# First attention of a two-layer decoder: weight folds and weight splits put first, latent matmuls in two halves, half of the key spreads by vector copies, last chunk projected tile by tile

## The reference, cut to what matters

```
xn = layernorm(x)
q  = (xn @ Wq_d + bq_d) @ W_qk + b_qk        # 12 latents -> 32 heads x 4
kv = xn @ Wkv_d + bkv_d                      # 4 latents, the same for all heads
p  = softmax(q . kv / sqrt(4))               # per sequence: 64 x 64, 32 heads
v  = kv @ Wv_u + bv_u                        # 4 -> 32 x 16
x  = x + (p v) @ Wo + bo
```

## Time and profile before

| | us |
|---|---|
| median of 3 runs (1344.39 to 1349.4) | 1345.4 |
| the profiled execution | 1349.59 |
| its span | 1347.8 |
| stage A in it (to VectorE's last instruction) | 206.7 |

### The profile page before, as it was taken

One profiled execution on the slowest core, in us unless ns is written; L12 is line 12 of the kernel. 1 busy time (PEld: TensorE's weight loads), 2 busy tenths in 40 slices (PEclk: granted clock), 3 DMA queues, 4 the chain that ended last, 5 costly groups with the idle time before them and its releaser, 6 DMA issues. The chain is left out here.

```text
span 1347.8 us, 24381 instructions
## 1 busy us (share of the span) xinstructions
PE 1148.2 (85%) x9342; PEld 606.5 (45%) x9342; DVE 759.5 (56%) x1316; ACT 416.6 (31%) x654; POOL 393.5 (29%) x318
## 2 busy tenths in 40 slices
PE   4798873988896979998999999999488769999993
PEld 2455441666663434443444444444354334444441
DVE  6756652688876876437514313512499822646466
ACT  4556741555541113411111211211233212222230
POOL 3334535888840000049200000000122200225052
PEclk8888855799998998998999999999699979999997
DMA  5000001111101004322000000000000000000000
GB/s 193 4 3 4 21 2 31 42 40 41 42 5 39 0 11 123 111 72 88 0 0 1 0 0 0 1 0 0 13 10 10 3 24 1 9 23 23 8 32 32
DMA packets 30634, 35.82 MB, mean 27 GB/s; under 512 B 7194, under 2 KB 21811, under 8 KB 30548
## 3 DMA queue, kind: packets, MB, share of 16 engines
q1 hardware_dynamic: 29810, 34.56, 8.2%
q10 hardware_dynamic: 738, 0.05, 0.0%
HBM read 30.10 MB, written 4.19 MB: 25 GB/s over the span
## 5 line engine op out<-in xcount | busy, mean ns | idle before, releaser
L1641 DVE TENSOR_TENSOR d_h_low<-d_hf,d_h_high 128x512 f16<-128x512 f32 (+1 forms) x40 | 32.6, 816 | 205.9 <-ACT d_h_high L1698 205.9
L109 PE MATMUL d_p_up<-d_xt_high,wd_hi 128*128 128x512 f16 (+1 forms) x352 | 134.1, 381 | 2.9 <-PE d_p_y L111 1.5
L110 PE MATMUL d_p_up<-d_xt_low,wd_hi 128*128 128x512 f16 (+1 forms) x352 | 133.9, 380 | 0.0
L111 PE MATMUL d_p_up<-d_xt_high,wd_lo 128*128 128x512 f16 (+1 forms) x352 | 133.9, 380 | 0.0
L109 PE MATMUL d_p_y<-wd_hi,d_h_high 128*128 128x512 f16 (+1 forms) x272 | 104.7, 385 | 3.1 <-DVE d_h_low L1641 3.1
L110 PE MATMUL d_p_y<-wd_lo,d_h_high 128*128 128x512 f16 (+1 forms) x272 | 104.8, 385 | 0.0
L111 PE MATMUL d_p_y<-wd_hi,d_h_low 128*128 128x512 f16 (+1 forms) x272 | 104.6, 385 | 0.0
L404 POOL TENSOR_TENSOR a_pt_low<-a_ex,a_pt_high 128x1024 f16<-128x1024 f32 x32 | 68.1, 2128 | 99.0 <-ACT a_pt_high L786 99.0
L151 ACT ACTIVATE d_sg<-d_p_up 128x512 f32<-128x512 f32 (+1 forms) x40 | 23.7, 593 | 211.8 <-PE d_p_up L111 211.8
L1837 POOL MEMSET e_wskip<- 128x128 f32 x1 | 0.2, 205 | 300.1 <-POOLq L1567 300.1
L2172 DVE TENSOR_TENSOR f_h_low<-f_sq,f_h_high 128x512 f16<-128x512 f32 x32 | 27.4, 857 | 71.0 <-ACT f_h_high L2244 71.0
(11 more groups left out here) (304 smaller groups left out, 2978.6 us busy)
## 6 DMA issues: line engine op xcount, KB each, us to landing
wd_raw<-in_w_d SPq DMA_DIRECT2D x16, 616.0 KB, 3.7
wd_raw<-in_w_f SPq DMA_DIRECT2D x8, 578.0 KB, 3.7
X<-in_x SPq DMA_DIRECT2D x4, 1024.0 KB, 9.4
b_kt<-in_ctx_t SPq DMA_DIRECT2D x128, 32.0 KB
out_x<-wd_raw SPq DMA_DIRECT2D x16, 256.0 KB, 2.0
b_cd<-in_ctx SPq DMA_DIRECT2D x32, 64.0 KB, 2.3
a_bd<-a_keys SPq DMA_DIRECT2D x72, 4.0 KB
wd_raw<-in_w_c SPq DMA_DIRECT2D x4, 274.0 KB, 5.1
```

The lines of the kernel that those rows point to most:

```text
L109: nc.tensor.matmul(ps, st[0], mv[0], start=start, stop=False)
L110: nc.tensor.matmul(ps, st[0], mv[1], start=False, stop=False)
L111: return nc.tensor.matmul(ps, st[1], mv[0], start=False, stop=stop)
L1641: nc.vector.tensor_tensor(hid[1][0:n, d % NH, :], value, hid[0][0:n, d % NH, :], ALU.subtract).then_inc(h_ready, 1)
```

## The change

- **Loads.** The sync queue now fetches x chunk 0, `Wo`, `bo`, x chunk 1, all of `w_c` in one transfer (its buffer holds all four pieces), x chunks 2 and 3. `Wv_u` and `bv_u` go first on ScalarE's queue.
- **Folds.** They are written into `p_st` (free until the first scores_t), in pieces between the first chunk's T, L, V and Q; the splits stand among the first query splits on VectorE.
- **Fillers.** `keep_warm(k)` issues k f16 matmuls of 512 columns into unused partitions of `p_m`: 14 at the very start, then `light(c, j)` of them before turn_top in units with little chunk work: 4, 2, 2, 2, 2 in units 2 to 6, 4 in each of units 10, 18, 23, 24, 25, 26 and 31 (54 in all).
- **Latents.** The four matmuls of L (chunks 1 to 3) are two in the unit's place and two after the following turn_top.
- **Key spreads.** Of 8 heads, 4 are written by VectorE (two copies after the peak of units j = 3 and 4, 12 in all) and 4 by 12 transfers for each chunk.
- **Weights of stage C** are split before the unit loop: ScalarE's four passes before its copy of L, VectorE's four after the first two norms of chunk 1.
- **Last chunk.** Z and O of chunk 3 become `Y` (transpose of one tile) and `P` (projection of one tile): Y0, P0 and Y1 in units 28, 30 and 31, P1 and Y2 after attend(30), P2 after attend(31), and Y3, P3 at the end.
- **VectorE and ScalarE at the start.** The second `bd` buffer is cleared later, the query weights are prepared after the first norms, and both `delta` passes (L788) stand before the first transposed tile is copied.

```diff
-        fold = {4: ("W", 0, 0), 6: ("W", 0, 1)}
+        last = {4: ("Y", NC - 1, 0), 6: ("P", NC - 1, 0), 7: ("Y", NC - 1, 1)}
...
-        final = [("Z", 0), ("O", 0), ("O", 1), ("O", 2), ("O", 3)]
+        after = {N: [("P", NC - 1, 1), ("Y", NC - 1, 2)], N + 1: [("P", NC - 1, 2)]}
+        final = [("Y", NC - 1, 3), ("P", NC - 1, 3)]
...
+        EARLY_WARM = 14
...
+        def light(c, j):
+
+            weight = sum({"T": 0.85, "L": 3.2, "Q": 0.3, "O": 0.64, "P": 0.64}.get(use[0], 0) for use in chunk_uses(c, j))
+            return max(0, math.ceil((0.5 - weight) / 0.16))
...
-                    for h in range(8):
+                    for h in range(4, 8):
                         for r in range(3):
...
+                def turn_y(i):
+                    pe.wait_ge(z_ready, TC * (NC - 1) + i + 1)
+                    for s in range(2):
+                        for g in range(2):
+                            r = slice(64 * g, 64 * g + 64)
+                            last = nc.tensor.matmul(bank(("Y", NC - 1, i))[r, 64 * s:64 * s + 64],
+                                                    z[r, i, s, :, :].rearrange("p h d -> p (h d)"),
+                                                    held.ident[r, r], start=True, stop=True)
+                    last.then_inc(zt_ready, 1)
...
+                def keep_warm(times):
+
+                    for _ in range(times):
+                        nc.tensor.matmul(p_m[0:96, :], held.ident16[:, 0:96],
+                                         held.ident16[:].rearrange("p (a n) -> p a n", a=1).broadcast_to([128, 4, 128]),
+                                         start=True, stop=True)
...
                     pe.wait_ge(mx_ready, n + 1)
                     pe.wait_ge(delta_ready, 1 if c == 0 else 2)
+                    if n == 0:
+                        pe.wait_ge(wvo_read, 3)
...
-                pe.wait_ge(pat, 4)
+                pe.wait_ge(id_ready, 1)
+                keep_warm(EARLY_WARM)
+                fold_wvo(range(0, 2))
                 for use in first:
+                    if use[0] == "V":
+                        fold_bvo(range(0, 2))
                     front(use)
+                    if use[0] == "T" and use[2] == 3:
+                        fold_wvo(range(2, 4))
+                    if use[0] == "L":
+                        latents(0, range(2, KB))
+                    if use[0] == "Q" and use[2] == 1:
+                        fold_bvo(range(2, 4))
...
+                        keep_warm(light(n // 8, n % 8))
...
+                    if n % 8 == 1 and n // 8 + 1 < NC and n < N:
+                        latents(n // 8 + 1, range(2, KB))
```

More of the change, by code:

```diff
@@ L270, in stage_a @@
         bvo_h = held.wd_lo[0:2, 0:D]
+        zl = [held.wd_lo[:, D + CH * w:D + CH * w + CH] for w in range(2)]
         wqk_raw = spare[:, 6 * D + 1536:6 * D + 1664].rearrange("p (g n) -> p g n", g=4)
@@ L585, in spread_values @@
                             ALU.mult).then_inc(wv_ready, 1)
+                    for o in range(4):
                         nc.vector.tensor_scalar(bv_rep[:, o, :], held.ones[:], bv_col[:, o:o + 1], None,
@@ L675, in after_peak @@
                         norm(c + 2, 1)
-                    if c == NC - 1 and 0 <= j < NP_C:
-                        low_weights(j)
+                    if c == NC - 1 and j == 7:
+                        update(c, 0)
+                        measure(c, 0)
+                    if more and j in (3, 4):
+                        spread(c + 1, range(2 * j - 6, 2 * j - 4))
                 nc.vector.memset(kq_raw, 0.0).then_inc(kq_clear, 1)
@@ L705, in _ @@
                 norm(1, 1)
+                for q in range(NP_C):
+                    low_weights(q)
                 for n in range(N + 2):
@@ L808, in _ @@
                 delta(0)
+                delta(1)
                 for use in first:
+                    if use[0] == "L":
+                        for q in range(NP_C):
+                            high_weights(q)
                     front(use)
-                    if use[0] == "L":
-                        delta(1)
                 shift(0)
@@ L902, in output, with output_last @@
                                      stop=True).then_inc(o_ready, 1)
-                def fold_weights(i):
-                    pe.wait_ge(wv_ready, 8)
-                    both = wv_bd if i == 0 else bv_rep
-                    for o in range(4):
-                        left = both[:, o, :, :].rearrange("p h d -> p (h d)") if i == 0 else both[:, o, :]
-                        last = nc.tensor.matmul(bank(("W", 0, i)), left, wo[:, o, :], start=o == 0, stop=i == 0 and o == 3)
-                    if i:
-                        last = nc.tensor.matmul(bank(("W", 0, i)), held.ones[0:1, :], bo, start=False, stop=True)
-                    last.then_inc(fold_ready, 1)
+                def output_last(i):
+                    tile = slice(128 * i, 128 * i + 128)
+                    pe.wait_ge(y_low, i + 1)
+                    mm3(nc, bank(("P", NC - 1, i)), [w[:, tile] for w in zl], [w[:] for w in held.wvo], True, False)
+                    nc.tensor.matmul(bank(("P", NC - 1, i)), held.units[:], held.bvo[:], start=False,
+                                     stop=True).then_inc(o_ready, 1)
@@ new lines, in fold_wvo, with fold_bvo @@
+                def fold_wvo(os):
+                    pe.wait_ge(par_b, 32)
+                    pe.wait_ge(wv_ready, 4)
+                    for o in os:
+                        last = nc.tensor.matmul(p_st[:, 0, :], wv_bd[:, o, :, :].rearrange("p h d -> p (h d)"),
+                                                wo[:, o, :], start=o == 0, stop=o == 3)
+                    if 3 in os:
+                        last.then_inc(fold_ready, 1)
+                def fold_bvo(os):
+                    pe.wait_ge(wv_ready, 8)
+                    for o in os:
+                        nc.tensor.matmul(p_st[:, 1, :], bv_rep[:, o, :], wo[:, o, :], start=o == 0, stop=False)
+                    if 3 in os:
+                        nc.tensor.matmul(p_st[:, 1, :], held.ones[0:1, :], bo, start=False, stop=True).then_inc(fold_ready, 1)
```

160 lines of the change are left out of this document (93 added, 67 removed).

## The result

The changed kernel takes **1336.5 us** (median; 1334.8 to 1340.4) beside 1344.7 us for the kernel before on the same chips: a ratio of 0.9943, 95% interval [0.9918, 0.9968]. So it is faster, by 7 to 8 us (the intervals reach from 4 to 11) where the forecast said 16.2. The time lies inside the forecast range, but half of the gain is missing.

A forecast was written before the change was run, and what follows sets the result against it. TensorE, through its fixed order and clock, was taken as the bound in the third chunk, waiting for others in the first and last. Terms -0.9 + 8.9 - 2.0 + 5.5 + 4.7 = 16.2 off 1345.4 gave 1329 us, range 1315 to 1340.

The forecast's parts named there:

- Start, +0.9: Stage A up to the first peak: 0.9 us later, with the added folds put where TensorE waits.
- First chunk, -8.9: Stage A's first chunk: 8.9 us less with the folds removed, VectorE being the next limit.
- Second and third chunk, +2.0: Stage A's middle chunks: 2.0 us lost together, from fillers, spread copies, transfers and clock falls.
- The copies as a whole: Key spread copies on VectorE: 2.4 us lost beside low_p in the middle chunks, 1.4 of VectorE's time in the first.
- Last chunk, -5.5: Stage A's last chunk, to the last attend: 5.5 us less, with weight splits gone and the clock up.
- Rival 2: Last chunk: clock falls in units 27 to 30, which have no fillers; 9.5 us less, 1336 us, chance 0.18.
- End, -4.7: Stage A behind the last attend: 4.7 us less, 7.9 to 9.7 us against 13.2.
- What stage A saves, the program saves: Behind stage A: no wait for the barrier or a load depends on the change, so the saving carries over whole.
- Rivals 3 and 4: Start: clock stays down; folds moved, not hidden, 1341 us, chance 0.10; or fillers never raise it, 1352 us, chance 0.07.
- Rival 5: Start: `Wo` lands late and TensorE starts 3 or more us late; 1333 us, chance 0.05.
- Rival 1: Stage A: clock stays up nearly throughout; 27.5 us less, 1318 us, chance 0.22.
- signs of a miss: First peak outside 31-38 us; clock 0.50 at L; last chunk 0.60 or less; middle chunks moving over 4 us.

The follow-up runs named there:

- e11: Changed kernel with the folds of Wo and bo and their splits back in units 4 to 7 of the first chunk: 1342.2 us, ratio 0.9990.
- e8: Changed kernel with all key spreads by DMA, e5's start order, mask passes ahead of rstd, fold splits after the first peak: 1333.9 us.
- e12: Changed kernel with all key spreads by DMA and 24 filler matmuls before the first scores of the second attention: 1330.7 us.
- e4: Changed kernel with all eight heads' keys spread by DMA in chunks 1 to 3, no VectorE copies there: 1329.0 us, ratio 0.9888.
- e15: Changed kernel with all key spreads by DMA and more fillers in TensorE's waits of the first three chunks: 1328.6 us.
- e14: Changed kernel with the four splits of stage C's weights back in the last chunk: 1345.3 us, ratio 0.9992.
- e3: Changed kernel without the 40 filler matmuls in the units, the 14 at the start kept: 1341.0 us, ratio 0.9975.
- e16: Kernel before, unchanged, profiled once more: 1344.8 us.
- e5: Changed kernel with its start reordered, statistics of chunk 0 first and each fold in one piece: 1334.9 us, ratio 0.9937.
- e7: Changed kernel without the 14 early fillers at the start: 1338.0 us.
- e13: Changed kernel with more fillers in TensorE's waits of the first three chunks, VectorE copies kept: 1338.7 us.
- e1: Kernel before, unchanged, profiled once more: 1349.2 us.
- e2: Changed kernel, unchanged, profiled and timed again: 1337.9 us, ratio 0.9945.

## Why the prediction was half right

- **Start, +0.9, measured +4.8 to +5.4: the step that failed.** I counted the folds as lying in TensorE's waits. e11 gives their price: 3.5 to 4.2 us. The trace has the last piece, at the half clock, and the splits that wait for it right in front of the first peak. The rest is small things put ahead of the statistics: the value pass behind a load (7.64 us). I had bounded this term by -2 to +10, and taken a value near its good end.
- **First chunk, -8.9, measured -8.0 to -9.1: right**, with the weight splits at 0.66 a piece (2.64 in all, 2.4 forecast) and VectorE busy in 33.7 of 38.8 us. e8 confirms the reason, that VectorE comes next. e11 gives the folds' share as 10.
- **Second and third chunk, +2.0: right in one trace (74.5), missed by 3.1 and 5.8 in the others (77.6, 80.3).** In stage A the copies cost 1.8 (forecast 2.4). I treated the clock as a won or lost fall at a known place. The traces show that waits of 0.6 to 1.9 us there may or may not bring it down, and that the falls at 102.5 and 143.5 us were new. My bound of 5 lost was too tight.
- **The copies as a whole were under-sized.** I gave them 2.4 us beside low_p, 1.4 of VectorE's time in the first chunk and a part of the 1.3 there, less the 0.6 us of waiting for transfers: some 4. Without them the medians are 5 to 10 us lower (e12, e4, e15, each against its sibling on the same chip). Stage A's traces show at most 4 of it, and what makes the rest is open. That e4 comes out at 1329.0, the forecast's own number, is luck: it has a start that is 4 us late.
- **Last chunk, -5.5, measured -7.7: right in cause, under-sized.** e14 shows that the moved splits carry it (10.2 us longer with them there), e3 that the fillers add about 2. Rival 2 (falls in units 27 to 30) did not happen: 0.93 up to the last peak.
- **End, -4.7, measured -4.5: right.**
- **"What stage A saves, the program saves": not shown, and of little use.** The length behind stage A is not fixed: 6.7 us come or go with the second attention's rise, in both kernels (e16, e5, e7, e13). The traces of before that I had (and e1) were of its longer kind. Stage A of e13 is 2.8 us under e2's and 5.5 under the mean, and the median is not lower. Whether the change itself gives 2 to 3 us back is open.
- Rivals 3 and 4, that the clock stays down at the start, are out: L took 3.60 us, even without the early fillers (e7). But rival 3's heading, that the folds are moved and not hidden, is right for the start's 4 us, by another cause. Rival 5 is out: the first fold began at 9.70 us, ahead of the first tile. Rival 1, the clock up nearly throughout, was made in e13's trace, and its time was not won. Two of my own signs of a miss came: the first peak after 38 us, and middle chunks that moved by more than 4 us in two of three traces. The Trainium skill's rule on transposes (page "TensorE: Matmul & The Clock Gate", section "Part 4: PE-mode transpose") would have had L at 6.2; since fold pieces stand around the transposes, the runs neither show nor refute the rule itself.

In sum, against 16.2 and with the means of the ledger's three traces: 4.1 lost at the start, 3.0 in the middle, 0.4 in the first chunk and the end, 2.2 won in the last chunk. That leaves 10.9 us in stage A (10.5 with the mean of before's three traces). The medians say 7 to 8; the last 2 to 3 us no run explains.

## What to carry to other kernels

Before counting a moved operation as hidden, write down which wait it fills and how long that wait is once everything else that was moved there stands in it too. The clock falls at other places from one execution to the next, in the changed stage and behind it, so look at several traces of either kernel, and at where their executions lie among all, before giving a stage a price; believe the medians before one trace. Taking work that another engine waits for out of a chain (the weight splits) was worth more here (e14: 8 us) than the clock fillers (e3: 3 us; e7: none).

## What was not expected of the hardware

- The granted clock differs between executions of one program at the same instruction: 1.00 and 0.50 in the same unit, after the same wait (0.64 and 0.63 us).
- 97 us of stage A at 1.00 instead of 0.8 (e13's trace) did not show in the median of the program.
- Without the 24 fillers, the clock of the second attention rose 26 to 28, 35 to 36 or 43 us after its first tile, and it was 163 to 164, 170 to 171 or 172 us long then.
- Two f16 copies on VectorE (96x512) took 0.60 us alone and 1.59 beside a GpSimd pass of 2.13 us; the first of them ended when that pass did.
